# Causal mask added by VectorE inside the maximum, and leaf-bias conversions moved behind the routing steps

## Chip, cores and metric

The kernel runs on one core of a Trainium2 chip. The metric is the device time of one execution in microseconds (us), and beside it stands one execution taken by the hardware profiler. TensorE multiplies matrices into PSUM (8 banks of 512 fp32 words in each of 128 partitions), VectorE and ScalarE read and write PSUM and SBUF, GpSimd (POOL) works on SBUF and issues indirect DMAs, and SyncE (SP) issues the plain DMAs.

## What is computed

A decoder of four layers works on x of 8 sequences x 256 tokens x 256 features with a context of the same size. Each layer adds a gated attention and a gated feed-forward part. Two of the eight parts matter here. The first is layer 0's attention with a causal mask, 16 heads of 16 features:

```python
attn = jnp.einsum('bhqd,bhkd->bhqk', q, k) / scaling
causal = 1.0 - jnp.tril(jnp.ones((S, S), jnp.float32))
attn = attn + causal * -1000000000.0
probs = jax.nn.softmax(attn, axis=-1)
out = jnp.einsum('bhqk,bhkd->bhqd', probs, v)
```

The second is layer 2's feed-forward part: three trees (q, k, v) of depth 4. Each token walks down a tree to one of 16 leaves, and the leaf's two-layer network gives its row; an attention over the three outputs follows.

```python
for _ in range(DEPTH):
    score = jnp.einsum('nd,nd->n', xf, node_w[cur]) + node_b[cur]
    cur = 2 * cur + 1 + (score >= 0).astype(jnp.int32)
hidden = relu(xf @ w1[leaf] + b1[leaf])
out = hidden @ w2[leaf] + b2[leaf]
```

## The kernel before

The program is a row of phases with a barrier between them: setup, then attention and feed-forward of each layer. Every engine has its own instruction list, written out by hand, and they meet on semaphores.

**Attention of layers 0 and 1 (`phase_heads`).** The work is laid out on a common clock of "units". Each of the 8 batches (sequences) takes 8 units; a table `AT` says in which unit, counted from the batch's first, its other steps come: keys and queries of the next pair of batches (K, Q, every second batch), turned maxima (NMT), values (V), weighted sums (AV), token-wise results (TOK), and so on. In each unit TensorE first makes two score tiles (`scores`, L883): 128 queries against up to 256 keys for two heads, in one PSUM bank. They serve only to find each row's maximum. The bank comes from a ring of four (`d_bank`), which VectorE frees with the semaphore `d_free` when it has reduced the tile (`maximum`, L715, a negated maximum into `nmax`). For the first 128 queries (units 0 to 3) only 128 keys are looked at in layer 0, for the others (units 4 to 7) 256. Ten units later TensorE makes the same scores transposed (`scores_T`, L912) and adds the negated maxima to them by a second matmul (L916); ScalarE takes the exponential (L675) and GpSimd zeroes what lies on the wrong side of the diagonal (`below_diagonal`, L585). In layer 0 the maximum must leave out the later keys, so after `scores_T` of the unit TensorE adds a mask to both score tiles (`mask`, L893): a bf16 matmul of the mask matrix `causal` with the identity `identb` onto the diagonal block of both heads. Only then does `d_full` let VectorE start. At the end of a batch VectorE copies the maxima in two halves (`both_halves`, L724 and L726); a batch in this text goes from one L724 to the next. The constants are made in `phase_setup` by GpSimd.

**Trees (`phase_trees`).** TensorE makes the 45 node scores of each of the 16 token tiles, together with a copy of its rows (`gate_rows`, L322 and L323), into one PSUM bank per tile. From tile 8 on a bank is needed again: TensorE waits on `gate_in`, which VectorE raises when it has added up four tiles' scores (L2381 and L2383), and VectorE waits on `r_in`, which ScalarE raises when it has copied a tile's rows out (L2589). VectorE then runs a chain of small steps (`step`, 36 in all) that chooses leaves and gives each row its place, GpSimd scatters the rows of three trees with 48 indirect DMAs (L2563), and SP loads them back in tiles of one leaf pair each (`load_rows_of`, L2525). A ring of 69 steps over these tiles follows (first TensorE line L2728). Meanwhile TensorE and ScalarE make layer 3's keys and values for four blocks of 512 tokens (`keys_of`, `values_of`; `keys_in` L2605, `values_in` L2599). The leaf biases b2 (6 rows x 2048) go in as three bf16 parts: ScalarE rounds (L2582), VectorE takes the rounded part away (L2371), ScalarE rounds the rest (L2584), VectorE again (L2373), and ScalarE a last time (L2586). SP waits for all of it (`part` 5), then copies two of the parts into place (L2519), and only then starts to wait for the first tree's scatters (`sent[0]`). The ring waits for `placed`. Before the change ScalarE and VectorE do these five steps first of all in the phase.

Of the kernel before, what the change touches and what calls it, by code (L numbers as in the profile page):

```python
# [19 lines left out]
P = 128  # L20
NBATCH, SEQ, D = 8, 256, 256
# [66 lines left out]
def decoder_kernel(nc, a, out):  # L88
    ctx = ExitStack()
    with ctx:  # L90
        places = {}

        def sb(name, shape, dt=F32):
            places[name] = -(-nc.sbuf_base // 32) * 32
            return ctx.enter_context(nc.sbuf_tensor(name, shape, dt))
# [57 lines left out]
        identb = sb("identb", [P, P], BF16)  # L153
        causal = sb("causal", [P, P], BF16)
# [19 lines left out]

        hT = hbuf[:, :].rearrange("p (f t) -> p f t", f=NF)
# [163 lines left out]
        def phase_setup():  # L339
# [11 lines left out]
            with nc.Block() as block:  # L351
# [20 lines left out]
                def _(pool):  # L372
# [7 lines left out]
                    pool.affine_select(out=identb[:, :], in_=ones, pattern=[[-1, P]], compare_op=ALU.is_equal, fill=0.0,  # L380
                                       base=0, channel_multiplier=1).then_inc(cst, 1)
# [6 lines left out]
                    pool.memset(rt[:, :, :, :].rearrange("p a b c -> p (a b c)"), 0.0).then_inc(cst, 1)  # L388
                    pool.wait_ge(cst, 5)
                    zeros = rt[:, 0, :, :].rearrange("p a b -> p (a b)")  # L390
                    pool.affine_select(out=causal[:, :], in_=zeros, pattern=[[-1, P]], compare_op=ALU.is_ge, fill=NEG,
# [40 lines left out]
                @block.tensor  # L432
                def _(pe):
                    pe.wait_ge(cst, 4)
                    with pe.Fori(0, NB) as blk:
                        for u in range(2):
                            pe.wait_ge(nrm.link, nrm.done(blk, 0))
                            wait(pe, kept[2 * u], blk)
                            transpose_pair(pe, 2 * u, xs4[:, 2 * u:2 * u + 2, :]).then_inc(turned, 1)
                            pe.wait_ge(ctx_in[u], blk * 16 + 16)  # L440
                            wait(pe, kept[2 * u + 1], blk)
                            transpose_pair(pe, 2 * u + 1, prob[:, u].rearrange("p a b s -> p (a b) s")).then_inc(turned, 1)


        def phase_heads(l, sync_tail):
# [102 lines left out]
            with nc.Block() as block:  # L548
# [160 lines left out]
                def _(dve):  # L709
                    def maximum(b, k):  # L710
                        qt, g, p = s_tile(k)
                        h = g * GH + 2 * p
                        dve.wait_ge(d_full, d_no["S", b, k] + 1)
                        bank = ps[:, d_bank("S", b, k), :].rearrange("p (h s) -> p h s", h=2)
                        ins = dve.tensor_reduce(nmax[:, b % 2, qt, h:h + 2], bank[:, :, 0:keys(qt)], AXX, ALU.max, negate=True)  # L715
                        ins.then_inc(d_free, 1)
# [75 lines left out]
                def _(pe):  # L792
# [79 lines left out]
                    def scores(b, j):  # L872
# [5 lines left out]
                        for k in (2 * j, 2 * j + 1):  # L878
# [5 lines left out]
                                            kmb[blk % 2][r, :, g, u * SEQ:u * SEQ + kk], start=True, stop=not causal_l)  # L884
                            if not causal_l:
                                ins.then_inc(d_full, 1)

                    def mask(b, j):

                        for k in (2 * j, 2 * j + 1):  # L890
                            qt, g, p = s_tile(k)
                            bank = ps[:, d_bank("S", b, k), :].rearrange("p (h s) -> p h s", h=2)
                            pe.matmul(bank[:, :, qt * P:(qt + 1) * P], identb[:, :], causal[:, :].unsqueeze(1).broadcast_to([P, 2, P]),  # L893
                                      start=False, stop=True).then_inc(d_full, 1)
# [30 lines left out]
                    for unit in units:  # L925
# [6 lines left out]
                        if causal_l and s_b is not None:  # L932
                            mask(s_b, j)
# [1288 lines left out]
        def phase_trees(sync_tail):  # L2222
# [135 lines left out]
            with nc.Block() as block:  # L2358
                @block.vector
                def _(dve):  # L2360
# [8 lines left out]
                    dve.wait_ge(ld_b2, 16)  # L2369
                    dve.wait_ge(part, 1)  # L2370
                    dve.tensor_tensor(b2x, b2x, b2T[0:NFLAG], ALU.subtract).then_inc(part, 1)  # L2371
                    dve.wait_ge(part, 3)
                    dve.tensor_tensor(b2x, b2x, b2_mid, ALU.subtract).then_inc(part, 1)  # L2373
# [75 lines left out]
                    assert count[0] == T_STEPS, count[0]  # L2449

# [128 lines left out]
                def _(act):  # L2579
                    act.wait_ge(blank, 1)  # L2580
                    act.wait_ge(ld_b2, 16)
                    act.activation(b2T[0:NFLAG], b2x, ACT.Identity).then_inc(part, 1)  # L2582
                    act.wait_ge(part, 2)
                    act.activation(b2_mid, b2x, ACT.Identity).then_inc(part, 1)  # L2584
                    act.wait_ge(part, 4)
                    act.activation(b2_low, b2x, ACT.Identity).then_inc(part, 1)  # L2586
# [4 lines left out]
                    act.activation(wvT, ps[:, 6, :].rearrange("p (k d) -> p k d", k=KD), ACT.Identity).then_inc(w_in, 1)  # L2591
                    act.wait_ge(ld_leafm, 16)
                    act.activation(leafm[0:NPART], leafm_ld, ACT.Identity).then_inc(leafm_in, 1)

# [14 lines left out]
                    for blk in range(NB):  # L2609
                        values_in(blk)  # L2610
                        keys_in(blk)
                    act.wait_ge(ld_b1, 16)
# [700 lines left out]
```

## Time and profile before

| | |
|---|---|
| median of 3 runs | 1648.39 us (1647.24 to 1649.98) |
| profiled execution | 1648.31 us, of which the span from first to last instruction 1646.6 us |
| mean granted TensorE clock | 0.935 of full speed |
| busy: PE, DVE, ACT, POOL | 86%, 42%, 39%, 29% of the span |
| layer 0's attention | about 50 to 263 us |
| start of the trees, up to the ring | 1197 to 1261 us |

PE is TensorE, PEld its weight loads, DVE VectorE, ACT ScalarE, POOL GpSimd, SPq SyncE's queue. Matmuls overlap and their ends are modelled, so that the starts of two neighbours say more than one duration. "Released by" (an arrow) names what ended the idle time ahead of an instruction.

### The profile page before, as it was taken

What the parts mean: (1) busy time and instruction counts of PE and PEld (TensorE: products, weight loads), DVE (VectorE), ACT (ScalarE), POOL (GpSimd) and SP (SyncE); (2) the same over time, 40 slices, a digit from 0 to 9 for tenths busy, and PEclk for the clock granted to TensorE, in tenths of its full rate; (3) what the DMA queues carried; (4) which work ended last, traced back from release to release, by engine and by line L of the source; (5) the groups of instructions that cost most, each with busy time, mean ns of one, the idle gap of its engine ahead of it and who ended that gap; (6) DMA issues with size and microseconds to landing.
All of it is one profiled execution on the core that took longest, in us unless ns stands there. A gap on an engine that the chain in (4) does not pass through costs nothing. (4 is left out here: it accounts for less than half of the span.)

```text
span 1646.6 us, 29379 instructions
## 1 busy us (share of the span) xinstructions
PE 1420.2 (86%) x9785; PEld 1139.1 (69%) x9786; DVE 696.3 (42%) x1884; ACT 640.7 (39%) x1437; POOL 484.9 (29%) x548
## 2 busy tenths in 40 slices
PE   4999987999999999699997899946568898777598
PEld 3467765799999986467775799934355677645487
DVE  3455543400000006267752400047842564649575
ACT  2344543144444432145653244421133444323352
POOL 2455551022222210223321022215307534221330
PEclk9999997999999999879998999977879999988799
DMA  5800004556566643000003656620035875010000
GB/s 166 262 1 2 2 2 155 164 174 198 196 205 201 193 142 112 0 1 2 1 1 95 206 179 205 205 66 0 0 128 163 268 220 182 20 52 1 1 25 26
DMA packets 111835, 173.72 MB, mean 106 GB/s; under 512 B 20315, under 2 KB 88557, under 8 KB 111225
## 3 DMA queue, kind: packets, MB, share of 16 engines
q1 hardware_dynamic: 101567, 144.26, 28.0%
q0 software_dynamic: 10176, 28.24, 4.8%
q8 instruction: 57, 0.93, 0.2%
q14 instruction: 35, 0.29, 0.1%
HBM read 133.06 MB, written 39.35 MB: 105 GB/s over the span
## 5 line engine op out<-in xcount | busy, mean ns | idle before, releaser
L715 DVE TENSOR_REDUCE nmax<-ps 128x2 f32<-128x512 f32 (+1 forms) x256 | 145.9, 618 | 122.0 <-PE ps L893 73.5
L1392 ACT ACTIVATE kT<-ps,b_sb 128x128 f32<-128x128 f32 x312 | 114.7, 368 | 155.7 <-PE ps L1501 134.6
L675 ACT ACTIVATE wbuf<-ps 128x512 f32<-128x512 f32 (+1 forms) x256 | 123.9, 542 | 91.9 <-PE ps L916 91.3
L1501 PEld LDWEIGHTS ps<-qT,wbuf 128*128 128x128 f32 x1248 | 145.4, 192 | 3.9 <-issue 1.9
L1501 PE MATMUL ps<-qT,wbuf 128*128 128x128 f32 x1248 | 145.7, 275 | 1.7 <-issue 1.7
L1511 PE MATMUL ps<-L0f_second,kT 128*128 x624 | 141.1, 379 | 0.0
L271 POOL TENSOR_TENSOR sm<-sm,mhalf 128x4 f32<-128x4 f32 (+1 forms) x40 | 43.8, 1094 | 313.1 <-DVE sm L266 313.1
L1511 PEld LDWEIGHTS ps<-L0f_second,kT 128*128 128x128 f32 x624 | 115.5, 190 | 14.1
L335 ACT ACTIVATE xnT<-ps 128x512 f32<-128x512 f32 (+1 forms) x64 | 37.1, 596 | 198.9 <-PE ps L312 96.5
L916 PE MATMUL ps<-nmT_r,sel_r 32*128 32x256 f32 (+1 forms) x512 | 109.6, 426 | 0.0
L1903 ACT ACTIVATE kT<-ps,b_sb 128x128 f32<-128x128 f32 x152 | 55.5, 368 | 72.8 <-PE ps L1984 62.8
L1340 POOL DMA_INDIRECT qT<-expert_rows,rowt x39 | 38.0, 974 | 148.7 <-PE ps L1490 106.4
L575 POOL TENSOR_SCALAR hbuf<-kT,sel 128x512 f32<-128x512 f32 x32 | 49.6, 1564 | 90.3 <-ACT kT L626 90.3
L883 PE MATMUL ps<-hbuf,qT 32*128 32x512 f32 (+1 forms) x256 | 69.9, 651 | 5.3 <-POOL hbuf L575 4.5
L1984 PEld LDWEIGHTS ps<-qT,wbuf 128*128 128x128 f32 x608 | 70.9, 192 | 3.1 <-ACT qT L1897 1.5
L1984 PE MATMUL ps<-qT,wbuf 128*128 128x128 f32 x608 | 71.3, 275 | 1.6 <-ACT qT L1897 1.1
L912 PE MATMUL ps<-qT,hbuf 32*128 32x256 f32 (+1 forms) x512 | 71.9, 380 | 0.0
L585 POOL TENSOR_SCALAR_AFFINE_SELECT wbuf<-wbuf 128x256 f32<-128x256 f32 x128 | 49.8, 410 | 68.1 <-ACT wbuf L675 66.7
L1994 PE MATMUL ps<-wbuf,kT 128*128 x304 | 68.8, 379 | 0.0
L912 PE MATMUL ps<-stage,hbuf 32*128 32x256 f32 (+1 forms) x512 | 68.6, 374 | 0.2 <-ACT nmT_r L636 0.2
L883 PE MATMUL ps<-hbuf,stage 32*128 32x512 f32 (+1 forms) x256 | 67.8, 573 | 0.0
L1233 DVE TENSOR_TENSOR oT<-ps,ts 128x256 f32<-128x256 f32 x20 | 8.5, 425 | 139.8 <-PE ps L1511 139.8
(442 smaller groups left out, 3115.3 us busy)
## 6 DMA issues: line engine op xcount, KB each, us to landing
wbuf<-in_L_w SPq DMA_DIRECT2D x66, 1024.0 KB, 5.2
tree_rows<-rt SPq DMA_DIRECT2D x3, 3151.0 KB, 27.4
prob<-tree_rows SPq DMA_DIRECT2D x69, 137.0 KB, 3.5
tree_outputs<-probT SPq DMA_DIRECT2D x69, 128.0 KB, 3.0
L0f_second<-in_L_w SPq DMA_DIRECT2D x8, 1024.0 KB, 11.9
ts<-in_L_b SPq DMA_DIRECT2D x58, 128.0 KB, 3.0
wbuf<-in_L_rec SPq DMA_DIRECT2D x3, 2048.0 KB, 10.8
expert_rows<-vbuf SPq DMA_DIRECT2D x2, 2048.0 KB, 11.2
```

What stands on the lines that cost most here:

```text
L585: pool.affine_select(out=diag, in_=diag, pattern=[[0, 2], [1, P]], compare_op=ALU.is_ge, fill=0.0, base=0, channel_multiplier=-1).then_inc ...
L675: act.activation(PT[:, k, :, q0:], ps[:, a_bank("ST", b, k), :].rearrange("p (h s) -> p h s", h=2)[:, :, q0:], ACT.Exp, scale=scale).then_ ...
L715: ins = dve.tensor_reduce(nmax[:, b % 2, qt, h:h + 2], bank[:, :, 0:keys(qt)], AXX, ALU.max, negate=True)
L883: ins = pe.matmul(bank[:, :, 0:kk], qTb[blk % 2][r, g, u * SEQ + qt * P:u * SEQ + (qt + 1) * P], kmb[blk % 2][r, :, g, u * SEQ:u * SEQ + k ...
L912: pe.matmul(out, kmb[blk % 2][r, e, g, u * SEQ + kt * P:u * SEQ + (kt + 1) * P], qTb[blk % 2][r, g, u * SEQ + q0:(u + 1) * SEQ], start=Tru ...
L916: ins = pe.matmul(out, sel_r[r, h:h + 1].broadcast_to([2 * HD, P]), nmT_r[b % 2][r, q0:], start=False, stop=True)
L1392: act.activation(hs[:, f, :], hidden(f), func, bias=b1_sb[:, v, f:f + 1]).then_inc(h_in, 1)
L1501: ins = pe.matmul(hidden(f), first[v][:, kk, f * P:(f + 1) * P], xgT[:, kk, :], start=(kk == 0), stop=(kk == KD - 1))
L1511: ins = pe.matmul(ps[:, 4 + v, 0:D], hs[:, f, :], second[:, ds(e, 1), f * D:(f + 1) * D][:, 0, :], start=(f == 0), stop=(f == NF - 1))
L1903: act.activation(hs[:, f, :], hidden(f), func, bias=b1_sb[:, v, f:f + 1]).then_inc(h_in, 1)
L1984: ins = pe.matmul(hidden(f), first[v][:, kk, f * P:(f + 1) * P], xgT[:, kk, :], start=(kk == 0), stop=(kk == KD - 1))
L1994: ins = pe.matmul(ps[:, 4 + v, 0:D], hs[:, f, :], second[:, ds(e, 1), f * D:(f + 1) * D][:, 0, :], start=(f == 0), stop=(f == NF - 1))
```

## The change

Two independent edits. **Mask.** `identb`, `causal` and the `mask` matmuls go. The first 256 words of the scratch tile `ts` become `seen`: 128 zeros, then the 128x128 mask. In layer 0 each score tile is now taken by two VectorE instructions, one for each head, which add the mask to the scores in place in PSUM, multiply by -1, and give the minimum of the row, which is the negated maximum. `d_full` is raised by the score matmul itself. Layer 1 keeps its reduction. **Leaf biases.** ScalarE's first rounding goes behind its copies of the rows and of the leaf masks, the second behind `keys_in(1)`, the third behind `keys_in(2)`; VectorE's two subtractions go behind the last routing step.

```diff
                     pool.memset(rt[:, :, :, :].rearrange("p a b c -> p (a b c)"), 0.0).then_inc(cst, 1)
+                    pool.memset(seen, 0.0).then_inc(cst, 1)
                     pool.wait_ge(cst, 5)
-                    pool.affine_select(out=causal[:, :], in_=zeros, pattern=[[-1, P]], compare_op=ALU.is_ge, fill=NEG,
+                    pool.affine_select(out=seen[:, P:SEQ], in_=seen[:, P:SEQ], pattern=[[-1, P]], compare_op=ALU.is_ge, fill=NEG,
...
-                        ins = dve.tensor_reduce(nmax[:, b % 2, qt, h:h + 2], bank[:, :, 0:keys(qt)], AXX, ALU.max, negate=True)
+                        if causal_l:
+                            kk = keys(qt)
+                            for e in range(2):
+                                ins = dve.tensor_tensor_reduce(out=bank[:, e, 0:kk], in0=bank[:, e, 0:kk], in1=seen[:, SEQ - kk:SEQ], scale=-1.0,
+                                                               scalar=BIG, op0=ALU.add, op1=ALU.min, accum_out=nmax[:, b % 2, qt, h + e:h + e + 1])
+                        else:
+                            ins = dve.tensor_reduce(nmax[:, b % 2, qt, h:h + 2], bank[:, :, 0:keys(qt)], AXX, ALU.max, negate=True)
...
-                                            kmb[blk % 2][r, :, g, u * SEQ:u * SEQ + kk], start=True, stop=not causal_l)
+                                            kmb[blk % 2][r, :, g, u * SEQ:u * SEQ + kk], start=True, stop=True)
+                            ins.then_inc(d_full, 1)
...
-                        if causal_l and s_b is not None:
-                            mask(s_b, j)
...
-                    dve.wait_ge(ld_b2, 16)
-                    dve.wait_ge(part, 1)
-                    dve.tensor_tensor(b2x, b2x, b2T[0:NFLAG], ALU.subtract).then_inc(part, 1)
-                    dve.wait_ge(part, 3)
-                    dve.tensor_tensor(b2x, b2x, b2_mid, ALU.subtract).then_inc(part, 1)
...
                     assert count[0] == T_STEPS, count[0]
+                    dve.wait_ge(ld_b2, 16)
+                    dve.wait_ge(part, 1)
+                    dve.tensor_tensor(b2x, b2x, b2T[0:NFLAG], ALU.subtract).then_inc(part, 1)
+                    dve.wait_ge(part, 3)
+                    dve.tensor_tensor(b2x, b2x, b2_mid, ALU.subtract).then_inc(part, 1)
...
                     act.activation(leafm[0:NPART], leafm_ld, ACT.Identity).then_inc(leafm_in, 1)
+                    act.wait_ge(ld_b2, 16)
+                    act.activation(b2T[0:NFLAG], b2x, ACT.Identity).then_inc(part, 1)
...
                         keys_in(blk)
+                        if blk == 1:
+                            act.wait_ge(part, 2)
+                            act.activation(b2_mid, b2x, ACT.Identity).then_inc(part, 1)
+                        elif blk == 2:
+                            act.wait_ge(part, 4)
+                            act.activation(b2_low, b2x, ACT.Identity).then_inc(part, 1)
```

## Rows read from the trace of the kernel before

**Rows 1.** Stretches of batches 3, 4: us; busy PE, PEld, DVE, ACT, POOL; clock, DMA.
```profile
99.66:126.91 27.25, 27.25 (x256) 18.09 (x254) 14.95 (x35) 12.65 (x27) 17.68 (x24) 1.00 0.01 1
126.91:147.86 20.95, 20.95 (x244) 15.62 (x242) 12.10 (x34) 10.43 (x24) 9.29 (x19) 1.00 0.00 1
```

**Rows 2.** Groups over the whole run: busy us, mean ns | idle before.
```profile
L715 DVE TENSOR_REDUCE nmax<-ps 128x2 f32<-128x512 f32 x192 | 121.9, 684 | 77.8 <-PE ps L883 47.7 <-PE ps L893 29.4
L715 DVE TENSOR_REDUCE nmax<-ps 128x2 f32<-128x256 f32 x64 | 24.0, 418 | 44.2 <-PE ps L893 44.2
L893 PE MATMUL ps<-causal,identb 128*128 128x256 bf16 x128 | 25.1, 278 | 0.0
L2381 DVE TENSOR_TENSOR hbuf<-ps,small 128x180 f32<-128x180 f32 x4 | 1.4, 346 | 9.8 <-ACT vbuf L2589 7.8 <-ACT stage L2589 2.0
L2655 ACT ACTIVATION_READ_ACCUMULATOR prob<-ps,negmax 128x1 f32 x16 | 3.5, 217 | 0.0
```

**Rows 3.** Timeline of TensorE in batch 4: start us, us, instructions.
```profile
131.91 0.47 PE L916 MATMUL ps<-nmT_r,sel_r 32*128 32x256 f32 x2
132.31 0.39 PE L893 MATMUL ps<-causal,identb 128*128 128x256 bf16 x2
132.63 0.48 PE L883 MATMUL ps<-hbuf,qT 32*128 32x256 f32 x2
...
133.94 0.39 PE L893 MATMUL ps<-causal,identb 128*128 128x256 bf16 x2
134.17 1.89 PE L863 MATMUL ps<-attw,oT 128*128 128x256 f32 x8
```

**Rows 4.** Timeline of TensorE in the second attention stage, which has no mask.
```profile
816.82 0.47 PE L916 MATMUL ps<-nmT_r,sel_r 32*128 32x256 f32 x2
817.22 1.99 PE L863 MATMUL ps<-attw,oT 128*128 128x256 f32 x8
...
820.06 0.47 PE L916 MATMUL ps<-nmT_r,sel_r 32*128 32x256 f32 x2
820.29 0.48 PE L912 MATMUL ps<-qT,hbuf 32*128 32x256 f32 x2
```

**Rows 5.** Timeline of VectorE in batch 0: first reductions and the last eight.
```profile
50.69 0.76 DVE L715 TENSOR_REDUCE nmax<-ps 128x2 f32<-128x256 f32 x2 [9.85 <-PE ps L893]
...
54.94 5.44 DVE L715 TENSOR_REDUCE nmax<-ps 128x2 f32<-128x512 f32 x8 [0.63 <-PE ps L893]
```

**Rows 6.** Timeline of the start of the tree stage, around the pause of TensorE.
```profile
1202.00 2.28 DVE L2371 TENSOR_TENSOR probT<-probT,attw 6x2048 f32<-6x2048 f32 x1 [8.43 <-ACT attw L2582]
1202.85 0.46 PE L323 MATMUL ps<-strip,xnT 128*128 128x173 f32 x2
1203.44 0.46 PE L323 MATMUL ps<-strip,xnT 128*128 128x173 f32 x2
1208.57 1.91 ACT L2586 ACTIVATE prob<-probT 6x2048 bf16<-6x2048 f32 x1 [2.35 <-DVE probT L2373]
1210.38 2.21 ACT L2589 ACTIVATE vbuf<-ps 128x256 f32<-128x256 f32 x8
...
1219.61 0.46 PE L323 MATMUL ps<-strip,xnT 128*128 128x173 f32 x2
```

**Rows 7.** Timeline of GpSimd: the first two of 48 scatters.
```profile
1236.36 1.42 POOL L2563 DMA_INDIRECT tree_rows<-vbuf,rowt  x1 [37.45 <-DVE rowt L2438]
1238.08 0.96 POOL L2563 DMA_INDIRECT tree_rows<-vbuf,rowt  x1 [0.30 <-issue]
```

**Rows 8.** Timeline of the last steps before the ring of tree steps.
```profile
1242.16 1.26 ACT L2605 ACTIVATE ctxT<-ps,cols 128x512 f32<-128x512 f32 x2
...
1258.49 2.74 SPq L2525 DMA_DIRECT2D prob<-tree_rows  x6
1259.00 1.26 ACT L2605 ACTIVATE ctxT<-ps,cols 128x512 f32<-128x512 f32 x2
...
1260.85 0.41 PE L2728 MATMUL ps<-ident,prob 128*128 128x128 f32 x2 [2.38 <-DMA prob<-tree_rows]
```

More of the change, by code:

```diff
@@ L152, in decoder_kernel @@
         ident = sb("ident", [P, P])
-        identb = sb("identb", [P, P], BF16)
-        causal = sb("causal", [P, P], BF16)
         hmask = sb("hmask", [P, GH])
@@ L173, in decoder_kernel @@
         ps = ctx.enter_context(nc.psum_tensor("ps", [P, 8, 512], F32))
+        seen = ts[:, 0, :]
         hT = hbuf[:, :].rearrange("p (f t) -> p f t", f=NF)
@@ L379, in _ @@
                                        base=0, channel_multiplier=1).then_inc(cst, 1)
-                    pool.affine_select(out=identb[:, :], in_=ones, pattern=[[-1, P]], compare_op=ALU.is_equal, fill=0.0,
-                                       base=0, channel_multiplier=1).then_inc(cst, 1)
                     with pool.Fori(0, NB) as blk:
@@ L388, in _ @@
                     pool.memset(rt[:, :, :, :].rearrange("p a b c -> p (a b c)"), 0.0).then_inc(cst, 1)
+                    pool.memset(seen, 0.0).then_inc(cst, 1)
                     pool.wait_ge(cst, 5)
-                    zeros = rt[:, 0, :, :].rearrange("p a b -> p (a b)")
-                    pool.affine_select(out=causal[:, :], in_=zeros, pattern=[[-1, P]], compare_op=ALU.is_ge, fill=NEG,
+                    pool.affine_select(out=seen[:, P:SEQ], in_=seen[:, P:SEQ], pattern=[[-1, P]], compare_op=ALU.is_ge, fill=NEG,
                                        base=0, channel_multiplier=1).then_inc(cst, 1)
@@ L433, in _ @@
                 def _(pe):
-                    pe.wait_ge(cst, 4)
+                    pe.wait_ge(cst, 3)
                     with pe.Fori(0, NB) as blk:
@@ L883, in scores @@
                             ins = pe.matmul(bank[:, :, 0:kk], qTb[blk % 2][r, g, u * SEQ + qt * P:u * SEQ + (qt + 1) * P],
-                                            kmb[blk % 2][r, :, g, u * SEQ:u * SEQ + kk], start=True, stop=not causal_l)
[L885 to L894, printed above, removed]
+                                            kmb[blk % 2][r, :, g, u * SEQ:u * SEQ + kk], start=True, stop=True)
+                            ins.then_inc(d_full, 1)
                     def scores_T(b, j):
@@ L2579, in _ @@
                 def _(act):
[L2580 to L2586, printed above, removed]
                     for t in range(NT):
@@ L2591, in _ @@
                     act.activation(wvT, ps[:, 6, :].rearrange("p (k d) -> p k d", k=KD), ACT.Identity).then_inc(w_in, 1)
+                    act.wait_ge(blank, 1)
                     act.wait_ge(ld_leafm, 16)
                     act.activation(leafm[0:NPART], leafm_ld, ACT.Identity).then_inc(leafm_in, 1)
+                    act.wait_ge(ld_b2, 16)
+                    act.activation(b2T[0:NFLAG], b2x, ACT.Identity).then_inc(part, 1)
                     def values_in(blk):
```

## The prediction

> **What bounds the kernel now.** The change touches two stages: the first attention stage (50 to 263 us), where the causal mask stands, and the start of the tree stage (1197 to 1261 us). I read the busy times by stretches first, cut at the VectorE copies that close each batch of the attention. In every such stretch TensorE's matmuls cover the whole time, at a granted clock of 1.00 (its 2.4 GHz level), while VectorE is busy 12.1 of 20.95 us in a batch without projections, and 14.95 of 27.25 us in one with them [rows 1]. So here a matmul taken away shortens the stage, and VectorE has some 8.9 us free in each batch. In the tree stage I read the timeline. There the ends are a chain through all engines: the gate matmuls, ScalarE's copies of their rows, VectorE's routing, GpSimd's scatters, the first loads, and then the ring of 69 steps. TensorE stops at 1203.9 us with eight banks full, because ScalarE, which must empty them, is inside the three conversions of the split leaf biases until 1210.4 us [rows 6].
>
> **The mask leaves TensorE.** The mask is two bf16 matmuls per unit, in 64 units (128 instructions) [rows 2]. What it costs is not its 278 ns but the distance by which it moves the next matmul. Where a projection or another block follows, the last L916 pair stands at 131.91 us, the mask pair 0.40 us later, and a following block 0.23 us behind its mask pair (133.94 to 134.17) [rows 3]. In the second attention stage, which has the same code with no mask, the distance from L916 to the next block is 0.40 us (816.82 to 817.22) [rows 4]. So the mask costs 0.23 us per unit. Where the next unit's scores follow at once (units 2 and 5 of batches 2, 4, 6 and 7: eight places), the distance is 0.72 us with it (131.91 to 132.63) and 0.23 without (820.06 to 820.29), so 0.49 us [rows 3, 4]. Batch 0 is apart (below). The other seven batches give 56 x 0.23 = 12.9 us, and 8 x 0.26 = 2.1 us more: 15.0 us.
>
> **The mask comes to VectorE.** A tile was one reduction of 512 or 256 elements; it becomes two instructions, each over one head's 256 or 128 elements, which read PSUM and an SBUF row, write PSUM, and also deliver a minimum. No row shows that instruction. Nearest below: a reduction of 256 elements. It takes 418 ns, and two in a row take 0.76 us [rows 2, 5], so they follow each other at 0.34 us; at (684 - 418) / 256 = 1.04 ns per element one of 128 elements follows at 0.21 us. An add of PSUM and SBUF does not show otherwise: one of 180 elements lasts 346 ns [rows 2], so one of 256 about 0.42 and one of 128 about 0.29 us. For the delivery of the minimum, the nearest row is ScalarE's, which shows it as an instruction of its own of 217 ns [rows 2]. I take 0.10 us for it, as about half of that overlapped: 0.44 us (long) and 0.31 us (short). The bound below is no delivery cost (0.34, 0.21); the bound above is no overlap at all (0.42 + 0.22 = 0.64, 0.29 + 0.22 = 0.51). With 16 long and 16 short ones, a batch costs VectorE 12.0 us (8.8 to 18.4), against 4 x 1.29 + 4 x 0.76 = 8.2 us now (0.61 us between two of 512 by the same arithmetic). With the other 3.9 us of such a batch that is 15.9 us, in a batch that TensorE would now do in 20.95 - 1.84 - 0.52 = 18.6 us. It fits, and each maximum starts earlier, since the tile is complete before the unit's transposed scores and not after them. But units 5 to 7 have the long tiles in short units, plus two token steps; with four banks I estimate 0.2 us of new waiting per batch, 1.5 us in all.
>
> The Trainium skill (VectorE: DVE Perf Modes, section "Two Vector instructions with no wait between them") says that an operation that also writes out its accumulator is two instructions on VectorE; no row of VectorE here shows one. It gives no duration for the read, and the sum above stands on the ScalarE row.
>
> **Batch 0.** Here no transposed scores run, and VectorE's reductions go from 50.69 to 60.38 us, 9.7 us, at TensorE's pace of scores and masks [rows 5]. With 12.0 us of new instructions VectorE becomes the bound: a loss of 2.3 us (a gain of 0.9 to a loss of 8.7). The stage gains 15.0 - 1.5 - 2.3 = 11.2 us. The changes to the constants in the setup are single GpSimd instructions beside its long input load: nothing, and at most 0.5 us if uncovered.
>
> **The leaf biases move.** ScalarE can now copy row tiles as they come. The gate matmuls of one tile take 0.59 us at the high clock (1202.85 to 1203.44), and ScalarE's eight held copies ran off in 2.21 us, some 0.28 us each; VectorE's two adds for the first four tiles (0.35 us each by the same group as above) are over before tile 8 asks for its bank at about 1203.9. So tiles 8 to 15 follow at once, the last matmul begins at 1203.44 + 8 x 0.59 = 1208.2 instead of 1219.61: 11.4 us earlier [rows 6]. Everything behind waits for these tiles and moves with them: routing, scatters (first at 1236.36), and the key and value projections, whose last ScalarE copy now ends at 1260.26, 0.6 us before the ring's first matmul [rows 7, 8]. What was moved must now hide. The first conversion (1.91 us) comes behind the last tile copy, while TensorE does the first keys. The second and third come behind the keys of blocks 1 and 2, where blocks follow each other at (1259.00 - 1242.16) / 2 = 8.42 us and ScalarE's key copies take 1.26 us and its two value copies as much again, so 1.91 us fits. The third ends at 1242.16 + 8.42 + 1.26 - 11.4 + 1.9 = 1242.3; the two copies that SP then issues have 4.8 us until SP would start the row loads (1258.49 - 11.4 = 1247.1) [rows 8]. VectorE's two subtractions (2.28 us each [rows 6]) lie in its empty time before the ring. So the stage keeps 11.4 us.
>
> **Sum.** 1648.3 us (the profiled execution: span 1646.6 and 1.7 around it; the median of the runs is 1648.4) less 11.2 and 11.4 is 1625.7, say 1626 us.
>
> **Rivals.**
> *A, the new instruction costs its full length* (0.64 and 0.51 us, or twice the time per element, since it reads and writes the same bank): 18.4 us per batch, with 3.9 beside it 22.3 us. Batches 2, 4, 6, 7 grow by 1.35 us each, 1, 3, 5 still gain 1.84, batch 0 loses 8.7: a loss of 8.6 in the stage, 1645 us. For it: nothing shows a VectorE write to PSUM; against: the add's 346 ns for 180 elements is no more than a plain reduction's.
> *B, slower:* the same mechanism further on. Beyond rival A each further us per batch is paid in all eight batches, so the stage's loss passes the trees' 11.4 us at 18.8 us per batch and the whole is slower by over 0.2% from 19.2 us, that is 0.60 us per instruction on average (my value 0.375). At 0.70 us, 22.4 us per batch, the stage loses 8.6 + 32 = 41 us: 1678 us.
> *C, the scatters are held:* the first scatter took 1.42 us, the next ones 0.96 us [rows 7], and the first stood beside a VectorE add of two SBUF inputs. Both subtractions now fall among the first tree's 16 scatters. If each holds them for its 2.28 us, the ring starts 4.6 us later: 1630 us. Late bias parts would look alike and cost at most 2 us. For it: that one row; against: it is also the first of its series.
> The Trainium skill (SBUF — State Buffer, "Who interferes with whom") speaks for C: a VectorE instruction with two SBUF inputs contends with a GpSimd instruction that reads SBUF. The same section infers that an add leaves descriptor generation alone, and then the time is the forecast's 1626 us.
> *D, the moved step does nothing for the end*, because the ring starts on something else (the keys' chain): 1637 us. Against: that chain starts from the same tiles.
>
> **Chances.** Forecast 0.66 (its own range 1621 to 1632: no delivery cost and no waiting give 15.9 + 11.4, thus 1621), A 0.12, B 0.07, C 0.12, D 0.03. Measurement can tell about 0.2% (3.3 us, so 1645) from no change: half of A's upper end lies inside. Faster 0.88, same 0.04, slower 0.08. For eight in ten the range is 1620 to 1641: it leaves out B and the upper part of A.
>
> **What the profile would show.** No L893; from L916 to the next block 0.40 us, and 0.23 to following scores; 512 new VectorE instructions that follow at 0.44 and 0.31 us, perhaps each with a short companion; batches without projections at about 18.6 us; batch 0 some 2 us longer. In the tree stage no pause after tile 7, last gate matmul about 11 us nearer to the first, scatters of 0.96 us throughout, and the ring's first matmul waiting for its load, not for the placed biases. Wrong would be: TensorE waiting long for the new instructions, or scatters of 2 to 3 us.

## The result, and the profile after

The changed kernel takes 1635.1 us (median of 4 runs, 1631.9 to 1636.2) where the one before takes 1648.1: by the medians 13 us faster. The ratio of all runs is 0.991 (95% interval 0.988 to 0.993). Forecast were 22.4 us and 1626 us. A repetition on another chip gave 0.992 (0.990 to 0.994). The profiled execution has a span of 1634.4 us, 12.2 less than before, at a mean granted clock of 0.924, which was 0.935. The 0.935 is at the upper end for the kernel before: its executions beside the experiments below have 0.919 to 0.935, with medians of 0.928 and 0.929.

**The mask.** Every instruction now has a companion that reads the accumulator. From the page's costliest groups and from VectorE's timeline in batch 0:

```profile
L715 DVE CUSTOM_DVE_ANT_0 ps<-ps,ts 128x128 f32<-128x128 f32 (+1 forms) x256 | 83.2, 391 | 45.7 <-PE ps L886 45.7
```

```profile
50.06 0.14 DVE L715 DVE_READ_ACCUMULATOR2_ANT nmax<- 128x1 f32 x1
50.06 0.33 DVE L715 CUSTOM_DVE_ANT_0 ps<-ps,ts 128x128 f32<-128x128 f32 x1
50.31 0.33 DVE L715 CUSTOM_DVE_ANT_0 ps<-ps,ts 128x128 f32<-128x128 f32 x1
...
54.26 0.47 DVE L715 CUSTOM_DVE_ANT_0 ps<-ps,ts 128x256 f32<-128x256 f32 x1
54.64 0.47 DVE L715 CUSTOM_DVE_ANT_0 ps<-ps,ts 128x256 f32<-128x256 f32 x1
```

The durations (0.33 and 0.47 us, and 0.14 for the read) overlap; what counts is the distance of two starts, 0.25 us with 128 elements and 0.38 with 256. TensorE's timeline in batch 4 answers to [rows 3]: the projection stands 0.40 us behind L910 (131.39 to 131.79), as in [rows 4]. Later in the batch is a new wait: L886 at 140.98 stretches, and L906 follows 0.87 us behind it; the same pair had 0.41 us before (L883 at 144.00, L912 at 144.41).

```profile
131.39 0.47 PE L910 MATMUL ps<-nmT_r,sel_r 32*128 32x256 f32 x2
131.79 1.99 PE L866 MATMUL ps<-attw,oT 128*128 128x256 f32 x8
...
140.98 1.46 PE L886 MATMUL ps<-hbuf,qT 32*128 32x512 f32 x3
141.85 0.67 PE L906 MATMUL ps<-stage,hbuf 32*128 32x256 f32 x3
```

By stretches, cut as in [rows 1], batches 3 and 4 have shrunk from 27.25 to 25.75 and from 20.95 to 19.12 us:

```profile
100.19:125.94 25.75, 25.75 (x246) 16.92 (x242) 17.34 (x83) 12.53 (x27) 17.80 (x24) 1.00 0.01 2
125.94:145.06 19.12, 19.11 (x234) 14.56 (x230) 14.78 (x83) 10.22 (x24) 9.02 (x19) 1.00 0.01 2
```

But look at batches 0 and 1, first of the kernel before, then of the one after. The column behind the five engines is the granted clock:

```profile
49.74:60.41 10.67, 10.67 (x56) 4.00 (x56) 8.18 (x17) 0.00 (x0) 0.00 (x0) 1.00 1.12 328
60.41:81.36 20.95, 20.95 (x162) 12.52 (x164) 8.51 (x19) 9.78 (x20) 13.00 (x17) 1.00 0.68 204
```

```profile
48.80:59.79 10.99, 10.31 (x34) 6.55 (x30) 10.32 (x65) 0.00 (x0) 0.00 (x0) 0.63 1.12 335
59.79:68.70 8.91, 8.91 (x30) 4.64 (x32) 3.62 (x26) 1.80 (x4) 0.00 (x0) 0.50 1.12 321
68.70:83.69 14.99, 14.98 (x131) 9.29 (x131) 7.54 (x40) 8.04 (x17) 13.07 (x18) 1.00 0.25 75
```

From 51.6 to 68.7 us TensorE has its lower level, 1.2 GHz. Batch 1 takes 23.90 us instead of 20.95; with the others' gain it would have taken 19.1.

**The trees.** The pause after tile 7 [rows 6] is gone: the last gate matmul begins 10.9 us after the first (1191.47 to 1202.41), which was 22.5. From the timelines of GpSimd, VectorE, SP's queue and TensorE:

```profile
1219.17 1.42 POOL L2555 DMA_INDIRECT tree_rows<-vbuf,rowt  x1 [25.86 <-DVE rowt L2425]
1220.89 2.91 POOL L2555 DMA_INDIRECT tree_rows<-vbuf,rowt  x1 [0.30 <-issue]
1224.10 0.96 POOL L2555 DMA_INDIRECT tree_rows<-vbuf,rowt  x1 [0.30 <-issue]
...
1229.15 1.99 POOL L2555 DMA_INDIRECT tree_rows<-vbuf,rowt  x1 [0.30 <-issue]
```

```profile
1220.68 2.28 DVE L2439 TENSOR_TENSOR probT<-probT,attw 6x2048 f32<-6x2048 f32 x1
1228.03 2.28 DVE L2441 TENSOR_TENSOR probT<-probT,prob 6x2048 f32<-6x2048 f32 x1 [5.07 <-ACT prob L2602]
```

```profile
1236.50 1.57 SPq L2511 DMA_DIRECT2D attw<-prob  x2
1244.17 1.85 SPq L2517 DMA_DIRECT2D prob<-tree_rows  x4
```

```profile
1247.04 0.66 PE L2722 MATMUL ps<-ident,prob 128*128 128x128 f32 x2 [5.76 <-DMA prob<-tree_rows]
```

The first scatter stands 27.7 us behind the first gate matmul, where it stood 39.3 [rows 7]: 11.6 gained. The two scatters beside the subtractions take 2.91 and 1.99 us. Each ends some 0.83 us behind its subtraction, as if it had done next to nothing until then. The ring begins 55.6 us behind the first gate matmul instead of 63.8: 8.2 gained. The parts of the leaf biases are copied long before SP's row loads (1236.5 against 1244.2).

**Where the 12.2 us are** (profiled executions, by the starts of the copy that closes a batch, of the first gate matmul and of the ring's first matmul):

| stretch | before | after | gain | forecast |
|---|---|---|---|---|
| start to the end of batch 0 | 60.41 | 59.79 | 0.6 | -2.3 |
| batch 1 | 20.95 | 23.90 | -2.95 | 1.6 |
| batches 2 to 7 | 136.24 | 125.93 | 10.3 | 11.8 |
| up to the trees' first gate matmul | 979.47 | 981.85 | -2.4 | 0 |
| to the ring | 63.78 | 55.57 | 8.2 | 11.4 |
| ring to the end | 385.75 | 387.36 | -1.6 | 0 |

### The profile page after: what moved, and what is told of

It is laid out like the page before. It is cut to its first block and busy times, and to the rows that moved or that the text cites. A ratio compares the mean times of both kernels' runs of the same rounds, so it can differ in the third digit from the quotient of the medians.

```text
span 1634.4 us, 29506 instructions
## 1 busy us (share of the span) xinstructions
PE 1416.4 (87%) x9657; PEld 1140.0 (70%) x9658; DVE 717.8 (44%) x2268; ACT 640.4 (39%) x1437; POOL 487.6 (30%) x548
## 5 line engine op out<-in xcount | busy, mean ns | idle before, releaser
L910 PE MATMUL ps<-nmT_r,sel_r 32*128 32x256 f32 (+1 forms) x512 | 109.7, 428 | 0.0
L715 DVE CUSTOM_DVE_ANT_0 ps<-ps,ts 128x128 f32<-128x128 f32 (+1 forms) x256 | 83.2, 391 | 45.7 <-PE ps L886 45.7
L718 DVE TENSOR_REDUCE nmax<-ps 128x2 f32<-128x512 f32 x128 | 80.4, 684 | 49.2 <-PE ps L886 49.1
L1895 ACT ACTIVATE kT<-ps,b_sb 128x128 f32<-128x128 f32 x152 | 55.6, 368 | 72.8 <-PE ps L1976 62.8
L886 PE MATMUL ps<-hbuf,qT 32*128 32x512 f32 (+1 forms) x256 | 73.8, 710 | 6.1 <-POOL hbuf L572 4.6
L906 PE MATMUL ps<-qT,hbuf 32*128 32x256 f32 (+1 forms) x512 | 71.8, 383 | 0.0
L1986 PE MATMUL ps<-wbuf,kT 128*128 x304 | 68.8, 379 | 0.0
L906 PE MATMUL ps<-stage,hbuf 32*128 32x256 f32 (+1 forms) x512 | 67.7, 373 | 0.2 <-ACT nmT_r L633 0.2
L886 PE MATMUL ps<-hbuf,stage 32*128 32x512 f32 (+1 forms) x256 | 67.5, 569 | 0.1
```

Source lines behind the costliest of these rows:

```text
L715: ins = dve.tensor_tensor_reduce(out=bank[:, e, 0:kk], in0=bank[:, e, 0:kk], in1=seen[:, SEQ - kk:SEQ], scale=-1.0, scalar=BIG, op0=ALU.ad ...
L886: ins = pe.matmul(bank[:, :, 0:kk], qTb[blk % 2][r, g, u * SEQ + qt * P:u * SEQ + (qt + 1) * P], kmb[blk % 2][r, :, g, u * SEQ:u * SEQ + k ...
L906: pe.matmul(out, kmb[blk % 2][r, e, g, u * SEQ + kt * P:u * SEQ + (kt + 1) * P], qTb[blk % 2][r, g, u * SEQ + q0:(u + 1) * SEQ], start=Tru ...
L910: ins = pe.matmul(out, sel_r[r, h:h + 1].broadcast_to([2 * HD, P]), nmT_r[b % 2][r, q0:], start=False, stop=True)
L1895: act.activation(hs[:, f, :], hidden(f), func, bias=b1_sb[:, v, f:f + 1]).then_inc(h_in, 1)
L1986: ins = pe.matmul(ps[:, 4 + v, 0:D], hs[:, f, :], second[:, ds(e, 1), f * D:(f + 1) * D][:, 0, :], start=(f == 0), stop=(f == NF - 1))
```

## Experiments

Twelve kernels ran, in four series, each beside the kernel before on the same chip. The ratio is to it, with its 95% interval; its own medians were 1649.2, 1649.5, 1649.0 and 1649.5 us, of which the table has the first. "Gap" is TensorE's idle time before the first scores of batch 0, "half clock" the stretch at a granted clock of 0.50 within batches 0 and 1, "ring" the time from the first gate matmul to the ring's first. These come from one profile of each kernel.

| kernel | median us | ratio | mask in batch 0 | gap | half clock | batch 1 | ring |
|---|---|---|---|---|---|---|---|
| before | 1649.2 | 1 | TensorE | 1.32 | none | 20.95 | 63.8 |
| after, again | 1637.3 | 0.992 (0.990 to 0.994) | VectorE | 1.75 | 54.4 to 71.4 | 23.88 | 55.5 |
| e_mask_only | 1643.6 | 0.996 (0.995 to 0.998) | VectorE | 1.43 | 52.7 to 69.8 | 24.38 | 64.1 |
| e_trees_only | 1642.1 | 0.995 (0.993 to 0.998) | TensorE | 0.87 | none | 20.95 | 55.7 |
| e_b0_on_pe | 1634.5 | 0.990 (0.988 to 0.992) | TensorE | 2.00 | 51.3 to 71.8 | 23.08 | 55.2 |
| e_filler | 1635.0 | 0.990 (0.988 to 0.992) | VectorE | 1.64 | 53.1 to 70.2 | 23.90 | 55.8 |
| e_gap_fill | 1638.1 | 0.993 (0.992 to 0.995) | VectorE | filled | 55.2 to 68.8 | 23.20 | 55.7 |
| e_keys_split | 1634.7 | 0.991 (0.989 to 0.993) | VectorE | 0.87 | 51.4 to 68.5 | 24.20 | 55.6 |
| e_sub_one_sbuf | 1633.0 | 0.989 (0.988 to 0.991) | VectorE | 1.62 | 52.7 to 69.8 | 24.11 | 52.4 |
| e_fill_both | 1633.6 | 0.991 (0.988 to 0.993) | VectorE | filled | 52.9 to 70.0 | 24.34 | 53.1 |
| e_b0_keys_early | 1633.0 | 0.990 (0.988 to 0.993) | TensorE | 0.87 | 60.2 to 67.0 | 22.97 | 54.5 |
| e_fill_rows | 1630.9 | 0.988 (0.985 to 0.992) | VectorE | filled | none | 20.19 | 53.2 |
| e_b01_pieces | 1629.6 | 0.987 (0.984 to 0.991) | TensorE | 0.87 | none | 20.94 | 52.7 |

### Each part alone

`e_mask_only` has the diff's first eight hunks, `e_trees_only` the other four.

> Only the mask moves to VectorE; the leaf biases stay where they were. My theory, from the trace after (the granted clock was 0.50 in batch 0 and the start of batch 1, and batch 1 took 23.9 us where its work asks for 19.1): the same dip, the second expert loads of the attention's end about 6.5 to 7 us earlier, and 1642 us (1640 to 1643.5). If the dip of the clock is chance and the mask is worth what I forecast (11.2 us), 1637 us. If the mask move alone is worth nothing and all of the gain is the trees', 1648 us.

> Only the leaf biases move; the mask stays on TensorE. My theory, that the two subtractions hold the scatters: first scatter 11.4 us nearer to the stage's first gate matmul, two scatters of some 2.9 and 2.0 us instead of 0.96, the ring's first matmul 8 us earlier, 1640 us (1639 to 1641.5). Forecast as it stood (scatters not held): 1637 us. If later stages give part of it back, between 1641 and 1644 us.

Both came out some two microseconds above my theory and just outside the ranges I gave (1643.6 where 1640 to 1643.5 was expected, 1642.1 where it was 1639 to 1641.5). By the ratios the mask is worth 6.3 us and the trees 8.1, together 14.4, where the whole has 13 to 15; no sign that one part disturbs the other. The trees' value also fits the third case of the expectation, that later stages give part back: in this profile the time from the ring to the end is 390.6 us, 4.8 more than in the kernel before. The half clock comes with the mask's move: in the profile with the mask alone it is there, in the one with the trees alone it is not, and the ring starts 8.1 us nearer to the first gate matmul with the two long scatters (2.91 and 1.98 us) and without a change to the mask.

### The scatters: one SBUF input instead of two

```diff
-dve.tensor_tensor(b2x, b2x, b2T[0:NFLAG], ALU.subtract)
+one = ps[0:NFLAG, 5, 0:1].broadcast_to([NFLAG, NPAIR * D])
+dve.tensor_tensor(b2x, b2x, one, ALU.subtract)
```

and the same for the second subtraction. This kernel leaves out what the split is for: the two lower parts of the biases no longer hold what the rounding lost.

> The kernel after, but the second operand of both subtractions is one PSUM column, broadcast; the subtractions keep their place and size and have one SBUF input instead of two. The lower parts of the split biases lose their meaning by it. Theory C, that two SBUF inputs hold GpSimd's scatters: all scatters behind the first 0.96 us, the ring's first matmul 3.0 us nearer to the first gate matmul (52.6 us instead of 55.6), 3 us below the kernel after. Rival: any VectorE instruction of 2.3 us beside a scatter does it (the first scatter of 1.42 us stands beside one of 0.73 us), scatters of 2.9 and 2.0 us as before, same time as the kernel after.

VectorE's and GpSimd's timelines of this kernel:

```profile
1221.80 2.28 DVE L2440 TENSOR_TENSOR probT<-probT,ps 6x2048 f32<-6x2048 f32 x1
1229.15 2.27 DVE L2442 TENSOR_TENSOR probT<-probT,ps 6x2048 f32<-6x2048 f32 x1 [5.08 <-ACT prob L2603]
```

```profile
1222.01 0.96 POOL L2556 DMA_INDIRECT tree_rows<-vbuf,rowt  x1 [0.30 <-issue]
1223.27 0.96 POOL L2556 DMA_INDIRECT tree_rows<-vbuf,rowt  x1 [0.30 <-issue]
...
1229.59 0.96 POOL L2556 DMA_INDIRECT tree_rows<-vbuf,rowt  x1 [0.30 <-issue]
```

Same place, same length, and no scatter is held. The ring starts at 52.4 us: 3.2 us are the price of the two second SBUF inputs. The rival, that any long VectorE instruction does it, falls. The first scatter takes 1.42 us here as well, and also in the kernels whose subtractions are in pieces; its cause is open, and it is no sign of this hold.

The Trainium skill (SBUF — State Buffer, "Who interferes with whom") says that a VectorE instruction with two SBUF inputs contends with a GpSimd instruction that reads SBUF, and one with at most one SBUF input, outside the two-port modes, does not; these runs agree, with 2.91 against 0.96 us. The same section infers that an add leaves descriptor generation alone; here the instruction that issues the scatter was held by a subtraction of the same form, and the measurement decides. Whether it was held in making its descriptors or in reading its index column from SBUF, these runs do not separate.

### The clock: four attempts that named the wrong thing

`e_b0_on_pe` leaves batch 0 to the mask matmuls and plain reductions (the constants and the `mask` matmuls come back for it):

```diff
-                        if causal_l:
+                        if causal_l and b > 0:
...
```

> The kernel after, but batch 0 alone keeps the mask matmuls and the plain reductions; batches 1 to 7 use the new instruction. Theory of the clock (a sparse TensorE in batch 0 loses the high level, and batch 1 pays for it): granted clock 1.00 from 50 us on, batch 1 of 19.1 us instead of 23.9, batch 0 no longer than 10.7 us, 1630 us (1628.5 to 1631.5). Rival, that batch 1 is long because VectorE's new instructions and the first transposed scores collide there: batch 1 stays at 23 to 24 us, and 1635 us.

`e_filler` keeps TensorE busier in batch 0, with this behind the scores of each unit:

```diff
+if causal_l and b == 0:
+    pe.matmul(ps[:, 4, 0:SEQ], qTb[0][0:2 * HD, 0, 0:P],
+              kmb[0][0:2 * HD, 0, 0, 0:SEQ], start=True, stop=True)
```

> The kernel after, with one more scores matmul of 256 columns per unit of batch 0, into a bank that nobody reads then; VectorE's work is unchanged. It is work without use. Theory of the clock: TensorE has no gaps in batch 0, the clock stays at 1.00, batch 0 keeps 10.9 us (VectorE's 10.1 and its start), batch 1 takes 19.1 us, 1630 us (1629 to 1632). Rival, that batch 0 and 1 are long because of VectorE: 1635 us or more, up to 1637 if the extra matmuls are in its way.

In both profiles the clock fell all the same, batch 1 took 23 to 24 us, and the medians were the 1635 us of the rivals. The rivals, that VectorE makes batch 1 long, are not refuted by this; what speaks against them is the granted clock of 0.50, and later `e_fill_rows`. Nor is the theory refuted for every execution: both profiles are of the slowest execution of their kernel (1642.5 and 1641.9 us). The mean granted clock of the other six of `e_b0_on_pe` is 0.926 to 0.930, between the 0.923 to 0.927 of the kernel after and the 0.928 to 0.933 of `e_trees_only`, so the clock may have held in some of them. TensorE's timeline and its windows in the profile of `e_b0_on_pe` show what was left, a long gap before the scores and a fall behind it, in a batch 0 that has all of its mask matmuls:

```profile
48.63 0.70 PE L893 MATMUL ps<-hbuf,qT 32*128 32x256 f32 x4 [2.00 <-POOL hbuf L579]
```

```profile
51.50:64.70 13.20, 13.20 (x36) 4.16 (x36) 6.66 (x13) 0.00 (x0) 0.00 (x0) 0.50 1.12 299
```

So the next series went for the gap. `e_gap_fill` puts five matmuls `pe.matmul(ps[:, 4, :], wq[:, 0, 0:P], xnT[:, 0, 0:BLK], ...)` behind the last query projection; `e_keys_split` shortens the wait itself, with GpSimd leaving this half to VectorE:

```diff
+if causal_l:
+    dve.wait_ge(consts, 1)
+    dve.wait_ge(a_free, a_no["K1", 0] + 1)
+    for e in range(2):
+        dve.tensor_scalar(kmb[0][:, e, 1, :], kT[:, 1, :], sel[:, H + e:H + e + 1], None, ALU.mult).then_inc(km_in, 1)
```

> The kernel after, unchanged, beside the others of this series, to compare with on one chip: ratio to the kernel before 0.991 (13 us), the mean granted clock of its executions 0.922 to 0.927, that is with the half-clock stretch at 52 to 69 us in nearly all of them.

> The kernel after, with five matmuls without use (512 columns, 0.43 us each) behind the last query projection of block 0, where TensorE waits some 1.4 to 2.0 us for GpSimd's masked keys before the first scores; batch 0 itself is as in the kernel after. Theory G, that this wait decides whether the clock falls (wait of 1.32 and 0.87 us: no fall; 1.43, 1.64, 1.73, 2.00: fall in the four other profiles): clock 1.00 through batches 0 and 1, batch 1 of 19.1 us, 4.5 us faster than the kernel after in executions that keep the clock, mean clock 0.930 or more. Rival V, that TensorE's waits for VectorE inside batch 0 decide: the clock falls all the same at 52 to 55 us and the time is that of the kernel after, within 1 us.

> The kernel after, but VectorE, idle there, makes the second half of block 0's masked keys beside GpSimd. Theory G: the wait before the first scores falls from 1.7 to about 0.8 us, the clock stays at 1.00, and the time is 4.5 + 0.9 = 5.4 us below the kernel after (1629 to 1631 where that is 1635). Rival V: 0.9 us below it and no more. If VectorE's instructions hold GpSimd's, the wait stays where it was.

Theory G, that the gap alone decides, falls too: with the gap filled or down to 0.87 us the clock still fell, at 55.2 and 51.4 us. (A filler took 0.86 us and not the 0.43 that I had read off a row with two records for each matmul, so five of them delayed the scores, and that kernel is not faster than the one after.) `e_keys_split` shortened the wait as hoped (0.87 us against 1.75), and its median is 2.6 us below the kernel after's.

### The clock: what the matmuls are

`e_fill_both` has the fillers of both sparse places (two behind the last query projection, one per unit of batch 0) and the subtractions in pieces:

```diff
-dve.tensor_tensor(b2x, b2x, b2T[0:NFLAG], ALU.subtract).then_inc(part, 1)
+for i in range(4):
+    c = slice(i * w, (i + 1) * w)
+    ins = dve.tensor_tensor(b2x[:, c], b2x[:, c], x[:, c], ALU.subtract)
+ins.then_inc(part, 1)
```

> The kernel after with two edits in places that don't touch each other. Attention: TensorE's work without use in both sparse places, two matmuls of 0.86 us behind the last query projection (before the first scores) and one of 256 columns per unit of batch 0. Neither place alone kept the clock. Theory GV, that the sum of the two sparse places loses the high level: clock 1.00 through batches 0 and 1, batch 1 of 19.1 us, 4.8 us less than the kernel after. Rival, that only the mask matmuls themselves or chance keep it: the clock at 0.50 again from 52 to 56 us on. Trees: each subtraction in four pieces of 512 columns. If the piece ends the hold, the two long scatters take under 1.5 us each and the ring starts up to 2.5 us nearer to the first gate matmul than 55.6 us; if the hold lasts as long as the pieces follow each other, 2.9 and 2.0 us and 55.6 us as before. Together 1628 us where the kernel after is 1635, 1630 with one of the two, 1635 with none.

`e_b0_keys_early` joins the edits of `e_b0_on_pe` and `e_keys_split`, and moves the first conversion and subtraction ahead of the routing, both on VectorE, ahead of the gate rows' adds and between them (ScalarE's second conversion moves up behind the leaf masks):

```diff
...
+dve.tensor_copy(b2T[0:NFLAG], b2x).then_inc(part, 1)
 for q in range(4):
...
+    if q < 2:
+        dve.wait_ge(part, 1)
+        c = slice(q * NPAIR * D // 2, (q + 1) * NPAIR * D // 2)
+        ins = dve.tensor_tensor(b2x[:, c], b2x[:, c], b2T[0:NFLAG, c], ALU.subtract)
```

> A kernel with useful work alone: batch 0 keeps its mask matmuls, VectorE makes half of block 0's masked keys, and the first conversion (on VectorE) and the first subtraction (in two halves between the adds of the gate rows) come before the routing. Theory GV: the wait before the first scores is 0.9 us, as it was 0.87 and 1.32 us in the two kernels that kept the clock, batch 0 is as dense as theirs, so the clock stays at 1.00, batch 0 takes 10.7 and batch 1 19.1 us: 5 us less than the kernel after. Trees: one long scatter (2 to 2.9 us) instead of two, first scatter at most 0.7 us later against the first gate matmul (27.7 us), ring start at 54 to 55 us. Together 1629 us where the kernel after is 1635. If the clock falls all the same, 1633 to 1634.

In `e_fill_both` TensorE has no idle time left. Its windows from 53 us on, over the rest of batch 0 and the start of batch 1:

```profile
53.00:60.16 7.16, 7.16 (x29) 5.87 (x25) 6.99 (x39) 0.00 (x0) 0.00 (x0) 0.50 1.12 336
60.16:69.80 9.64, 9.64 (x36) 5.20 (x36) 3.63 (x26) 2.15 (x4) 0.28 (x1) 0.50 1.12 332
```

Busy throughout, half clock throughout: theory GV is refuted as well. The kernel before had shown the same in its second attention stage, which has no mask, from 2 us behind its first scores on:

```profile
699.20:719.70 20.50, 20.50 (x64) 11.70 (x64) 13.35 (x23) 2.67 (x5) 2.10 (x2) 0.50 0.00 1
```

All fourteen profiles have this stretch of 20.5 or 23.9 us. It could have been read before the prediction, which took two distances from this stage and not its clock. `e_b0_keys_early` gave the hint. With the mask pairs in batch 0 and a gap of 0.87 us the clock held through batch 0 and fell at 60.2 us, 1.7 us behind the last mask pair (it ends at 58.50), where batch 1 begins with scores alone. Scores matmuls work on 32 rows of the array (the rows print 32*128); the mask pair works on 128. Hence `e_fill_rows` (the diff is against `e_fill_both`; the mask's constants are made again), and beside it `e_b01_pieces`, which has `b > 1` where `e_b0_keys_early` has `b > 0`, and its last subtraction in pieces:

```diff
-                        if causal_l and b == 0:
-                            pe.matmul(ps[:, 4, 0:SEQ], qTb[0][0:2 * HD, 0, 0:P], kmb[0][0:2 * HD, 0, 0, 0:SEQ], start=True, stop=True)
+                        if causal_l and 8 * b + j < 10:
+                            for _ in range(2):
+                                pe.matmul(ps[:, 4, 0:2 * P].rearrange("p (h s) -> p h s", h=2), identb[:, :],
+                                          causal[:, :].unsqueeze(1).broadcast_to([P, 2, P]), start=True, stop=True)
```

> As e_fill_both, with one difference: the matmul without use in the units of batch 0 (and of the first two units of batch 1) isn't a scores matmul on 32 rows of the array, but the former mask pair itself, bf16 on all 128 rows, into a bank that nobody reads then. VectorE still does the mask; TensorE's stream in batch 0 is that of the kernel before. Theory R, that matmuls on 32 of 128 rows alone don't hold the high level, however closely they follow, and those on 128 rows do: clock 1.00 through batches 0 and 1, batch 1 of 19.1 us instead of 24.3, 5 us below e_fill_both. Rival T, that the fall has to do with when the high level began (it came 9.9 to 13.8 us after the rise in every profile without masks in batch 0): half clock from 52 to 56 us on again, batch 1 of 23 to 24 us and the time of e_fill_both.

> As e_b0_keys_early, but batches 0 and 1 both keep their mask matmuls and plain reductions (in e_b0_keys_early the clock held through batch 0 and fell at 60.3 us, where batch 1 begins without masks), and the last subtraction is in four pieces. Theory R: clock 1.00 to the end of batch 1, batch 1 of 20.95 us as in the kernel before, instead of 22.97: 2.0 us less. Ring start 52.5 to 53 us after the first gate matmul instead of 54.5: 1.6 us less. Together 3.6 us below e_b0_keys_early, 1629.5 us. If the clock falls in batch 0 or 1 all the same (rival T), the time is that of e_b0_keys_early less 1.6.

The windows of `e_fill_rows`, batch 0 and the start of batch 1:

```profile
50.46:61.69 11.23, 11.23 (x56) 4.37 (x56) 10.30 (x64) 0.00 (x0) 0.00 (x0) 1.00 1.13 292
61.69:70.00 8.31, 8.31 (x51) 4.55 (x54) 4.62 (x34) 3.28 (x7) 2.48 (x2) 1.00 1.11 303
```

VectorE does the same work in batch 0 as in `e_fill_both` (10.30 us here), TensorE is as busy, the batch lasts as long (11.2 and 11.4 us), and the clock stays at 1.00; batch 1 takes 20.19 us instead of 24.34. It isn't 19.1; two of its units hold mask pairs without use, which is part of the 1.1 us, and the rest was not followed. The pair differs from the filler of `e_fill_both` in its rows (128 and not 32) but also in its type (bf16 and not fp32) and its values, and these three were not tried one by one. In batches 2 to 7 of the kernel after the clock is 1.00 without any bf16 matmul, so bf16 is not needed for it. The mean granted clock of whole executions says the same over more of them: 0.923 to 0.928 in six of `e_fill_both`, 0.927 to 0.934 in six of `e_fill_rows`, 0.920 to 0.927 in the twelve of `e_mask_only`. The kernel before, beside the first two of them, had medians of 0.929 and 0.928. The times of the two (ratios 0.988 and 0.991) have overlapping intervals, so the 4 us are shown in the profiles and not by the run times.

`e_b01_pieces` is the version with useful work alone: mask pairs in batches 0 and 1, the masked keys split, the first conversion and subtraction moved onto VectorE between the gate rows' adds, the last subtraction in pieces. Its windows are those of the kernel before:

```profile
48.79:59.47 10.68, 10.68 (x56) 4.01 (x56) 8.17 (x17) 0.00 (x0) 0.00 (x0) 1.00 1.12 304
59.47:80.41 20.94, 20.94 (x168) 12.56 (x170) 8.50 (x18) 9.78 (x20) 12.99 (x17) 1.00 0.82 228
```

The pieces worked too. GpSimd's timeline of `e_fill_both`:

```profile
1222.04 1.31 POOL L2567 DMA_INDIRECT tree_rows<-vbuf,rowt  x1 [0.30 <-issue]
...
1229.97 1.33 POOL L2567 DMA_INDIRECT tree_rows<-vbuf,rowt  x1 [0.30 <-issue]
```

Each subtraction takes 2.5 instead of 2.3 us and holds its scatter for 0.35 us instead of 1.95 and 1.03: a scatter gets its turn between two pieces. The ring starts at 53.1 instead of 55.6 us. With the first subtraction early it is 54.5 us (one long scatter left), with both edits 52.7.

`e_b01_pieces` has the lowest median here, 1629.6 us, 20 us below the kernel before. It was not timed beside the kernel after on one chip; by the ratios to the kernel before (0.987 against 0.991 and 0.992) it is 5 to 8 us below it, and its interval (0.984 to 0.991) overlaps theirs. That it beats the kernel after is thus likely and not shown.

## Why the prediction was right, and where it was off

- **The price of the new instruction** was an estimate, 0.44 and 0.31 us; it is 0.38 and 0.25. A batch costs VectorE 16 x 0.38 + 16 x 0.25 = 10.1 us and not 12.0. Rivals A and B fall. I took the read of the accumulator as 0.22 us, half hidden; it is 0.14 us and starts with the next instruction, wholly hidden. (There are 256 new instructions, 32 per batch as in the sum, and not the 512 of my list of signs.)
- **The distances on TensorE** were right: 0.40 us to the next block, and 10.3 us for six batches against 11.8. Without waits 1.84 to 2.36 us per batch were to come, 1.49 to 1.85 came. The difference of 0.3 to 0.6 us per batch, where 0.2 was estimated, I put down to new waits for VectorE; the one followed above took 0.46 us, the others were not.
- **Batch 0** went from 10.67 us to 11.67 (from the first scores at 48.12 to 59.79), a loss of 1.0 us and not 2.3, for the cheaper instruction. That the batch still ended 0.6 us earlier is luck: it comes from where the first scores fell (48.12 and not 49.74 us); over the fourteen profiles that varied from 46.4 to 50.9 us with equal code ahead of it in most of them.
- **The step that failed in the attention: "a matmul taken away shortens the stage", at a granted clock of 1.00.** I had read the clock in batches without the start of the stage and took it as given for all. The mask pairs were not only 0.23 us per unit of work; in batches 0 and 1, where few other matmuls on 128 rows run, the high level went with them. Without them batch 1 takes 4.8 us more than its 19.1. It is the largest term that was missing.
- **Tree stage.** The 11.4 us up to the first scatter came (11.6), the conversions hid as costed, and rival C, to which I gave 0.12, came with them at 3.2 us (4.6 was its price if each scatter waited a whole subtraction). Its mechanism is shown. The rule was in hand, and I gave more weight to the inference that spoke against it. The row that I had for it, the 1.42 us of the first scatter [rows 7], turned out to be no evidence, since that scatter takes 1.42 us with a PSUM operand too.
- **The rest.** 2.4 us were lost between batch 7 and the trees, and 1.6 in and behind the ring, in code that did not change. Ring to end took 382.9 to 390.9 us over the fourteen profiles, with no order by kernel but with one by the clock: where the half clock covers 63 to 68 us of it, it took 382.9 to 387.2 us, where it covers 76 to 80 us, 390.5 to 390.9. The kernel before has 63.3 us of it and the one after 73.4, so the 1.6 us are no price of the edit that these runs show. The stretch before took 979.3 to 982.3 us, and the profiles without mask pairs in batch 0 lie at its upper end (981.1 to 982.3, against 979.3 to 981.2 with them); In this stretch, too, the kernel before spent less time at half clock (125.8 us) than the one after (139.7). Whether that is a lasting loss, and by what, was not tried.

The sum of the differences: 2.9 - 4.6 - 1.5 - 2.4 - 3.2 - 1.6 = -10.4, which is 22.6 less 12.2. The sign held, and so did the eight-in-ten range (1620 to 1641 us); the forecast's own range (1621 to 1632) did not. Both parts work as the prediction says, the mask in batches 2 to 7 and the trees up to the first scatter; the size was off by two costs that lie on neither edit's own list, one of the clock (4.6 us) and one of a neighbour engine (3.2 us), and 2.9 us of too much caution in batch 0 hid part of it.

## What to carry to other kernels

Before taking matmuls on all 128 rows out of a stretch, look at what remains there: if it is short contractions (32 rows here), reckon with the lower clock, also for the code behind, look for such a stretch elsewhere in the trace, and try the edit with the first batches left as they were. When a VectorE instruction is moved, list what GpSimd does in its new place; with two SBUF inputs it holds an indirect DMA's issue for its whole length, and cutting it into pieces, or one operand from PSUM, gives most of that back. Sum the forecast by stages and compare by stages: here two errors of 3 to 5 us would have hidden in a total that lies inside the range.

## What the runs showed of the hardware

- TensorE ran at a granted clock of 0.50 for 17 us with no idle time in its rows (`e_fill_both`), in the first 8 us on matmuls of 32 rows alone, and for 20.5 us in the second attention stage of the kernel before; it ran at 1.00 with mask pairs of 128 rows among them (`e_fill_rows`, `e_b01_pieces`, `e_trees_only` and the kernel before). A gap of 2.00 us ahead of such a mixed stretch was followed by a fall all the same, and 13.2 us of scores with mask pairs then ran at 0.50 (`e_b0_on_pe`); gaps of 0.87 and 1.32 us were not followed by one. So the mask pairs are not enough by themselves. For the gap this rests on one profile each, that of `e_b0_on_pe` of its slowest execution, and a series over its length was not run.
- An add that writes its result back to PSUM and delivers a row minimum starts every 0.25 us with 128 elements and every 0.38 us with 256; the separate read of the accumulator lasts 0.14 us. A plain reduction of 256 elements starts every 0.34 us [rows 2, 5], so the add, the write to PSUM and the separate read together add some 0.04 us to it.
- A scatter beside a 2.28 us subtraction of two SBUF inputs took 2.91 us, beside the same one in four pieces 1.31 us, and beside one with a PSUM operand 0.96 us.
